# Attention's transposed outputs: copied by ScalarE, scaled by GpSimd, and GpSimd's weight work spread between

## The chip, the cores and the metric

One core of a Trainium2 chip runs the whole program in one launch. The metric is the device time in microseconds; lower is better.

## The reference

The input x has 8 sequences of 256 tokens with 512 features, and so has the context. One layer is computed, all in f32:

```python
x = x + xattn(layernorm(x), ctx, ctx, Wq, Wk, Wv, Wfc, bfc)   # 32 heads of 16, 8 groups of keys and values
x = x + ffn(layernorm(x), ...)                                # 8 experts, the best 2 in 2 of 4 groups, and a shared one

# in xattn, for each head
score = einsum('bhqd,bhkd->bhqk', qh, kh) / sqrt(HEAD_DIM)
attn = softmax(score, axis=-1)
out = einsum('bhqk,bhkd->bhqd', attn, vh)
return out.reshape(N, S_, EMBED) @ Wfc.T + bfc
```

The softmax is where the change lies: the kernel sums the exponentials with a column of ones beside the values, and divides the output by that sum at the end.

## The kernel before

**Stages.** Up to about 103 us in the profile the projections of q, k and v are computed and written to DRAM as pairs of f16 parts. Then comes the attention loop, to about 290 us. Then, tile by tile of 128 tokens (`TILES` is 16), the output projection, the second norm and the gate run. The expert network follows, with the weights held in SBUF as pairs of f16 parts.

**The attention loop.** It has 16 units (4 blocks of 512 tokens by 4 slices of the features, `UNITS`), each with 4 groups G (`UG`). A group is one key head with its four query heads over one sequence of 256 tokens; two groups that follow each other are a pair, so there are 32 pairs, two in each unit. Every engine has its own program over G, and each runs in order:

- TensorE (L1347 to L1385): four score fills per group (`score_fill`, L1304), each into bank 4 or 5; four fills for the row maxima of the unit after the next (`max_fill`, L1232; none in the last two units); the products with the values (`pv_part`, L1318) into bank 6; and in every odd group `pair_transpose(G - 3)` (L1335), four transposes of a finished pair into bank 7. Once per unit the row maxima are transposed into a part of bank 7 too (L1243). A score fill waits for the exp two fills before it.
- ScalarE (L1021 to L1032): four exps per group (L1028), then `attn_out(G - 1)` (L1014), a copy of a group's output from bank 6 into one of four buffers, `o_raw`.
- VectorE (L1854 to L1880): two reductions per group for the row maxima (`reduce`, L1701), the negated maxima once per unit (`neg_max_part`, L1758, L1761), and in every odd group `normalise(G - 3)`: the reciprocals of the sums in bank 7 (L1828) and the multiply of bank 7 by them into `attn_u` (L1830). In the last two units the reductions give way to the largest magnitudes of the down weights (`dn_abs_max`, L1838), each of which waits for a load into one of three ring buffers.
- GpSimd (L844 to L850): ten halves of the expert weights are cut in two f16 parts (`cut_weights`), each by three instructions over 128x1408: scaled and rounded (L818), scaled in place (L801), and the rest (L811); a half waits for `nm_done`, so there is about one per unit. After each comes one of 16 tiles to which the bias is added: `load_x(t + 1)` (L833), the add (L838) and the store (L840). `load_x(t)` waits until the store of tile t - 2 has landed, as they have two buffers. After ten halves the last six tiles follow one on the other.
- SyncE (L521 to L560): for each unit the negated maxima are stored into the q buffer (`nm_rows`, L511), twelve loads bring q and k of a later unit (`load_unit`, L475 and L479), and `store_attn` (L517) writes a finished unit's output to DRAM once `attn_done` says that both its pairs are normalised. From unit 12 on, the ring loads of the down weights (`load_ring`, L460) stand between these, `load_ring(9)` behind `store_attn(14)`. Its queue is in order: a store that waits holds up what stands behind it. At unit 15 the residual rows' load waits until all of one parity's attention stores have landed.

**After the loop** TensorE waits for `attn_done` of all groups (L1388) and begins the output projection of tile 0 (transposes L1397, products L1405). VectorE goes on with the tenth down-weight maximum and then the first tile's sum and norm (L1894 on). GpSimd waits for the last maximum before it loads the held weights (L792).

The functions that the diff touches:

Of the kernel before, what the change touches and what calls it, by code (L numbers as in the profile page):

```python
# [26 lines left out]
ALU = mybir.AluOpType  # L27
# [53 lines left out]
def build(nc, x, ctxT, wqT, wkvT, wfcT, bfc, gwT, wgu, wdn, out):  # L81
# [17 lines left out]
    with ExitStack() as ctx:  # L99
# [53 lines left out]
        assert at <= P3_0  # L153
# [92 lines left out]
        o_rec = small(2 * NM, TPB * HPG).rearrange("p (a h) -> p a h", a=TPB)  # L246
# [98 lines left out]
        ot_ready = sem("ot_ready")  # L345
# [51 lines left out]
        TOTAL = PA + PB + PC  # L397

# [348 lines left out]
        def _(pool):  # L747
# [66 lines left out]
            def cut_weights(c):  # L814
# [4 lines left out]
                scale_weights(c)  # L819
                second_part(c)  # L820
                if c + 2 < CUTS_P2:
                    load_cut(c + 2)
# [21 lines left out]
            for t in range(TILES):  # L844
                if t < CUTS_P2:
                    pool.wait_ge(nm_done, t + 3)
                    cut_weights(t)
                if t + 1 < TILES:
                    load_x(t + 1)
                add_bias(t)  # L850

# [66 lines left out]
        def _(act):  # L918
# [96 lines left out]

            exp_by = [nc.scalar.alloc_register(f"exp_by{n}") for n in range(BLOCKS)]
# [4 lines left out]
            for G in range(UNITS * UG):  # L1021
# [8 lines left out]
                if G > 0:  # L1030
                    attn_out(G - 1)
            attn_out(UNITS * UG - 1)  # L1032

# [140 lines left out]
        def _(pe):  # L1174
# [149 lines left out]
            def pair_transpose(G):  # L1324

                pe.wait_ge(pv_evac, G + 2)
                if G == 0:
                    pe.wait_ge(scale_done, 1)
                else:
                    pe.wait_ge(attn_done, G)  # L1330
# [16 lines left out]
            for G in range(UNITS * UG):  # L1347
# [22 lines left out]
                if j == 0 and has_next:  # L1370
                    if G > 0:
                        pe.wait_ge(attn_done, G - 2)
# [15 lines left out]
            pe.wait_ge(attn_done, LAST + 1)  # L1388
# [254 lines left out]
        def _(dve):  # L1643
# [177 lines left out]
            def normalise(G):  # L1821

                u, g = G // UG, G % UG // UB
                dve.wait_ge(ot_ready, G // 2 + 1)
                if g == 0:
                    dve.wait_ge(attn_st[u % 2], u // 2 * 16 + FREE)
                src = bank[7].rearrange("p (a h c) -> p a h c", a=TPB, c=VW)
                nc.vector.reciprocal(o_rec, src[:, :, :, HD]).then_inc(rec_done, 1)  # L1828
                dve.wait_ge(rec_done, G // 2 + 1)
                nc.vector.tensor_tensor(  # L1830
                    attn_u[u % 2][:, :, g * HPG * HD:(g + 1) * HPG * HD].rearrange("p a (h d) -> p a h d", d=HD),
                    src[:, :, :, 0:HD], o_rec.unsqueeze(3).broadcast_to([P, TPB, HPG, HD]),
                    ALU.mult).then_inc(attn_done, UB)
# [636 lines left out]
```

## Time and profile before

| what | us |
|---|---|
| median of 3 runs | 791.03 |
| lowest and highest run | 786.33 and 792.75 |
| the profiled execution | 788.99 |
| its span in the trace | 787.2 |
| TensorE, VectorE, ScalarE, GpSimd busy | 752.7, 580.6, 412.7, 269.9 |

The profiled execution's time is the span and 1.8 us around it. Busy time of TensorE is modelled, so a high share does not say that it runs at its peak. The mean granted clock of TensorE was 0.993 of full speed.

### The profile page before, as it was taken

To read this page: it belongs to the slowest core of one execution; us is meant where nothing else is said; L and a number is where in the kernel's file an instruction comes from. 1 tells how busy PE (TensorE), PEld (TensorE's weight loads), DVE (VectorE), ACT (ScalarE), POOL (GpSimd) and SP (SyncE) were. 2 spreads that over 40 slices of the span, in tenths; PEclk is the share of its full clock that TensorE was granted. 3 is DMA by queue.
4 is the path that set the end of the run, shared out by engine and by line. 5 is a ranking of instruction groups with operands and counts; after the bars stand their busy time and mean duration, and the time that the engine had idled before them with its cause. 6 is when DMAs were issued, how large, how long until landed. Compare 5 with 4: busy or idle time off the path is not lost.

```text
span 787.2 us, 15941 instructions
## 1 busy us (share of the span) xinstructions
PE 752.7 (96%) x5151; PEld 406.3 (52%) x5152; DVE 580.6 (74%) x1194; ACT 412.7 (52%) x843; POOL 269.9 (34%) x224
## 2 busy tenths in 40 slices
PE   6998989999998989999999999999999999998997
PEld 4553534344333335655655655555555555554553
DVE  5767789899998876999789886555555555545667
ACT  3665578798888863555534553343434334232231
POOL 3362008999993302556100101111111111033431
PEclk9999999999999999999999999999999999999999
DMA  8998856656646799996678566776777777569985
GB/s 318 358 394 239 251 159 207 188 158 206 188 123 181 261 330 324 333 386 219 184 240 228 124 148 156 173 186 174 177 177 176 184 173 176 124 194 255 276 246 152
DMA packets 161784, 172.09 MB, mean 219 GB/s; under 512 B 103680, under 2 KB 117504, under 8 KB 161216
## 3 DMA queue, kind: packets, MB, share of 16 engines
q1 hardware_dynamic: 150012, 128.89, 56.9%
q0 software_dynamic: 11120, 41.43, 17.3%
q10 hardware_dynamic: 596, 1.07, 0.4%
q8 instruction: 31, 0.51, 0.3%
q14 instruction: 25, 0.20, 0.1%
HBM read 105.40 MB, written 42.73 MB: 188 GB/s over the span
## 4 chain that ended last, share of the span: by engine, by line
PE 64%; DVE 16%; DMA 8%; SPq 4%; issue 4%; ACT 2%; ACTq 0%; DVEq 0%
PE psum L1469 28%; PE psum L1481 15%; PE psum L1318 6%; PE psum L1304 4%; PE psum L1208 4%; PE psum L1232 3%; DMA sb_weights<-k_parts 2%; DMA sb_hT<-sb_h 2%; DMA sb_weights<-in_wdn 2%; SPq L475 2%; PE psum L1405 1%; DVE sb_rows L1904 1%; SPq L479 1%; DVE sb_rows L1701 1%; DVE sb_stats L1896 1%
## 5 line engine op out<-in xcount | busy, mean ns | idle before, releaser
L1469 PE MATMUL psum<-sb_weights,sb_rows 128*128 (+1 forms) x1608 | 251.7, 313 | 0.0
L1469 PEld LDWEIGHTS psum<-sb_weights,sb_rows 128*128 128x128 f16 x1608 | 157.6, 98 | 92.1 <-issue 0.5
L1701 DVE TENSOR_REDUCE sb_rows<-psum 128x4 f32<-128x1024 f32 x128 | 150.4, 1215 | 9.9 <-PE psum L1232 9.8
L1028 ACT ACTIVATE sb_weights<-psum 128x512 f32<-128x512 f32 x256 | 139.8, 595 | 27.7 <-PE psum L1304 24.8
L1481 PE MATMUL psum<-sb_weights,sb_hT 128*128 (+1 forms) x630 | 148.3, 381 | 3.3 <-DMA sb_hT<-sb_h 3.3
L892 POOL DMA_INDIRECT sb_rows<-xn_rows,sb_slot_tok x39 | 38.4, 984 | 218.3 <-DVE sb_rows L2290 147.8
L1481 PEld LDWEIGHTS psum<-sb_weights,sb_hT 128*128 128x128 f16 x630 | 61.5, 98 | 68.9 <-DMA sb_hT<-sb_h 4.1
L1097 ACT ACTIVATE psum<-psum 128x352 f32<-128x352 f32 x71 | 31.8, 448 | 113.5 <-DVE psum L1951 113.5
L1304 PE MATMUL psum<-sb_weights 50*128 50x512 f16 x256 | 86.3, 386 | 2.7 <-ACT sb_weights L1028 1.4
L1318 PE MATMUL psum<-sb_weights 128*32 128x256 f32 x1024 | 82.5, 395 | 0.3
L1232 PE MATMUL psum<-sb_weights 48*128 48x256 f16 x512 | 69.9, 273 | 5.2 <-DMA sb_weights<-k_parts 4.4
L912 POOL DMA_INDIRECT sb_weights<-slot_y,sb_p_i x32 | 31.8, 995 | 83.7 <-DMA slot_y<-sb_rows 39.8
L1951 DVE SCALAR_TENSOR_TENSOR psum<-psum,sb_inv_now,sb_h 128x352 f32<-128x352 f32 x39 | 23.1, 593 | 49.3 <-PE psum L1469 49.3
L1405 PE MATMUL psum<-sb_weights 128*128 128x512 f32 x128 | 58.9, 603 | 0.1
L1964 DVE SCALAR_TENSOR_TENSOR sb_h<-psum,sb_h_scale_i,sb_h 128x352 f16<-128x352 f32 x71 | 41.3, 582 | 18.8 <-ACT sb_h L1102 18.6
L1304 PEld LDWEIGHTS psum<-sb_weights 50*128 50x128 f16 x256 | 23.4, 93 | 55.1 <-ACT sb_weights L1028 43.8
L1092 ACT ACTIVATE sb_h<-psum,sb_inv_now 128x352 f32<-128x352 f32 x39 | 21.6, 553 | 55.5 <-PE psum L1469 55.5
L1208 PE MATMUL psum<-sb_weights 128*128 128x512 f16 x192 | 44.9, 380 | 3.9 <-issue 2.6
L1102 ACT ACTIVATE sb_h<-psum,sb_h_scale_i 128x352 f16<-128x352 f32 x71 | 39.3, 553 | 17.6 <-DVE sb_h_scale_i L1956 17.6
L801 POOL TENSOR_TENSOR sb_weights<-sb_weights,sb_w_scale_i 128x1408 f32<-128x1408 f32 x15 | 38.5, 2570 | 27.7 <-ACT sb_weights L1070 26.9
L1092 ACT ACTIVATE sb_h<-psum,sb_w_inv_i 128x352 f32<-128x352 f32 x32 | 17.7, 554 | 54.2 <-PE psum L1469 40.4
L811 POOL TENSOR_TENSOR sb_weights<-sb_weights 128x1408 f16<-128x1408 f32 x15 | 42.9, 2859 | 1.2
(266 smaller groups left out, 1018.2 us busy)
## 6 DMA issues: line engine op xcount, KB each, us to landing
sb_weights<-in_wgu SPq DMA_DIRECT2D x20, 704.0 KB, 7.6
sb_weights<-in_wgu POOLq DMA_DIRECT2D x20, 704.0 KB, 5.6
sb_weights<-in_wdn SPq DMA_DIRECT2D x17, 768.0 KB, 5.7
slot_y<-sb_rows SPq DMA_DIRECT2D x39, 256.0 KB, 2.3
sb_weights<-q_parts SPq DMA_DIRECT2D x96, 64.0 KB, 2.5
x_dram<-sb_rows SPq DMA_DIRECT2D x24, 256.0 KB, 4.3
q_parts<-sb_weights SPq DMA_DIRECT2D x16, 256.0 KB, 4.4
sb_rows<-in_x POOLq DMA_DIRECT2D x16, 256.0 KB, 4.6
```

Of the source, the lines that this page charges most:

```text
L811: nc.gpsimd.tensor_tensor(low, stage, high, ALU.subtract).then_inc(gu_cut, 1)
L1028: nc.scalar.activation(probs[G % 2][:, kt, pair * 512:(pair + 1) * 512], bank[4 + f % 2], ACT.Exp, scale=exp_by[n]).then_inc(exp_done, 1)
L1092: nc.scalar.activation(silu_out[par], two_parts(bank[GU_BANKS[par][0]]), ACT.Silu, scale=inv).then_inc(sil_done, 1)
L1208: mm = nc.tensor.matmul(bank[Q_BANKS[n][m]], wq16[:, wp, k, m * P:(m + 1) * P], xnT[n % 2][:, xp, k, :], start=(k == 0 and i == 0), stop=( ...
L1232: mm = nc.tensor.matmul(bank[banks[qt] + side][:, h * SEQ:(h + 1) * SEQ], q_st[s][lo:hi, g, h, b * SEQ + qt * P:b * SEQ + (qt + 1) * P], k ...
L1304: nc.tensor.matmul(bank[4 + side].rearrange("p (h t) -> p h t", h=HH), k_st[s][lo:hi, g, b * SEQ + kt * P:b * SEQ + (kt + 1) * P], q_st[s] ...
L1318: mm = nc.tensor.matmul(bank[6][VW * c:VW * (c + 1), 0:SEQ], v_now, probs[G % 2][:, kt, c * SEQ:(c + 1) * SEQ], start=(kt == 0), stop=(kt ...
L1405: mm = nc.tensor.matmul(bank[2 + s][:], oT[s][:, k, :], wfc_sb[:, k, :], start=(k == 0), stop=(k == KD - 1))
L1469: mm = nc.tensor.matmul(bank[GU_BANKS[par][which]][:, 0:F], x_T[:, xp * D + k * P:xp * D + (k + 1) * P], gu(wp, k, which), start=(k == 0 a ...
L1481: mm = nc.tensor.matmul(bank[Y_BANKS[par]][:], hT[par][:, hp, j, :], dn(wp, j), start=(j == 0 and n == 0), stop=(j == NF - 1 and n == 2))
L1701: nc.vector.tensor_reduce(to[:, :, j // UB, :, j % UB, qt], psum[:, banks[qt] * 512:(banks[qt] + 2) * 512] .rearrange("p (a h k) -> p a h ...
L1964: nc.vector.scalar_tensor_tensor(h16[par][:, 1, 0:F], bank[GU_BANKS[par][1]][:, 0:F], h_scale[:, par:par + 1], h16[par][:, 0, 0:F], ALU.mu ...
```

## The change

ScalarE copies bank 7 whole, after a pair's transposes, into one of two new SBUF buffers `o_t` (`copy_pair`). VectorE takes the reciprocals from there, into one of two small buffers (`sums`), a group later than before. GpSimd multiplies (`normalise`). TensorE waits for the copy, where it waited for the normalised pair. GpSimd's 30 cut steps and 16 bias tiles are placed by a table between the multiplies: two or three steps and one or no tile per unit up to unit 12, then three tiles in unit 13, four in unit 14.

```diff
+        o_t = [words(at + s * D, D).rearrange("p (a h c) -> p a h c", a=TPB, c=VW) for s in range(2)]
-        o_rec = small(2 * NM, TPB * HPG).rearrange("p (a h) -> p a h", a=TPB)
+        o_rec = [small(at, TPB * HPG).rearrange("p (a h) -> p a h", a=TPB) for at in (2 * NM, 424)]
+        PAIRS = UNITS * UG // UB
...
# GpSimd
+            def cut_step(i):
+                c = i // 3
+                if i % 3 == 0:
+                    first_part(c)
+                elif i % 3 == 1:
+                    scale_weights(c)
+                else:
+                    second_part(c)
+                    if c + 2 < CUTS_P2:
+                        load_cut(c + 2)
+            def normalise(p):
+                u, g = p // MG, p % MG
+                pool.wait_ge(rec_done, p + 1)
+                pool.wait_ge(ot_copied, p + 1)
+                if g == 0:
+                    pool.wait_ge(attn_st[u % 2], u // 2 * 16 + FREE)
+                nc.gpsimd.tensor_tensor(
+                    attn_u[u % 2][:, :, g * HPG * HD:(g + 1) * HPG * HD].rearrange("p a (h d) -> p a h d", d=HD),
+                    o_t[p % 2][:, :, :, 0:HD], o_rec[p % 2].unsqueeze(3).broadcast_to([P, TPB, HPG, HD]),
+                    ALU.mult).then_inc(attn_done, UB)
...
-            for t in range(TILES):
-                if t < CUTS_P2:
-                    pool.wait_ge(nm_done, t + 3)
-                    cut_weights(t)
-                if t + 1 < TILES:
-                    load_x(t + 1)
-                add_bias(t)
+            done_cuts = done_bias = 0
+            for u in range(UNITS):
+                cuts = (3 if u in (2, 5, 8, 11) else 2) if u < 13 else 0
+                biases = {2: 0, 5: 0, 8: 0, 11: 0, 13: 3, 14: 4, 15: 0}.get(u, 1)
+                for i in range(cuts):
+                    if i == 1 and u > 0:
+                        normalise(2 * u - 1)
+                    cut_step(done_cuts)
+                    done_cuts += 1
+                if cuts == 0:
+                    normalise(2 * u - 1)
+                for i in range(biases):
+                    if done_bias + 1 < TILES:
+                        load_x(done_bias + 1)
+                    add_bias(done_bias)
+                    done_bias += 1
+                normalise(2 * u)
+            normalise(PAIRS - 1)
...
# ScalarE
+            def copy_pair(p):
+                act.wait_ge(ot_ready, p + 1)
+                if p >= 2:
+                    act.wait_ge(attn_done, UB * (p - 1))
+                nc.scalar.copy(o_t[p % 2], bank[7].rearrange("p (a h c) -> p a h c", a=TPB, c=VW)).then_inc(ot_copied, 1)
                 if G > 0:
                     attn_out(G - 1)
+                if G % 2 == 1 and G > 2:
+                    copy_pair((G - 3) // 2)
             attn_out(UNITS * UG - 1)
+            copy_pair(PAIRS - 1)
...
# TensorE: pair_transpose, the maxima's transpose, after the loop
-                    pe.wait_ge(attn_done, G)
+                    pe.wait_ge(ot_copied, G // UB)
-                        pe.wait_ge(attn_done, G - 2)
+                        pe.wait_ge(ot_copied, (G - 2) // UB)
-            pe.wait_ge(attn_done, LAST + 1)
+            pe.wait_ge(ot_copied, PAIRS)
...
# VectorE
+            def sums(p):
+                dve.wait_ge(ot_copied, p + 1)
+                if p >= 2:
+                    dve.wait_ge(attn_done, UB * (p - 1))
+                nc.vector.reciprocal(o_rec[p % 2], o_t[p % 2][:, :, :, HD]).then_inc(rec_done, 1)
-                if j % 2 == 1 and G > 2:
-                    normalise(G - 3)
+                if j % 2 == 0 and G > 3:
+                    sums((G - 4) // 2)
...
+            sums(PAIRS - 2)
             dn_abs_max(2 * UG)
-            normalise(UNITS * UG - 2)
+            sums(PAIRS - 1)
             dn_abs_max(2 * UG + 1)
```

## Rows read from the trace of the kernel before

**Rows 1.** Busy time by stretch: stretch, length, engines, TensorE clock, DMA share, GB/s
```profile
115.00:260.00 145.00, 140.03 (x1518) 56.72 (x1518) 135.79 (x177) 122.61 (x250) 119.37 (x83) 0.99 0.60 177
260.00:289.00 29.00, 27.46 (x258) 9.84 (x254) 23.57 (x28) 24.75 (x51) 4.21 (x5) 1.00 0.94 328
```

**Rows 2.** Timeline of ScalarE in the last two units: start, length, instruction, idle before
```profile
273.63 2.31 ACT L1028 ACTIVATE sb_weights<-psum 128x512 f32<-128x512 f32 x4
...
276.67 2.16 ACT L1028 ACTIVATE sb_weights<-psum 128x512 f32<-128x512 f32 x4 [0.46 <-PE psum L1304]
...
279.12 2.31 ACT L1028 ACTIVATE sb_weights<-psum 128x512 f32<-128x512 f32 x4
...
286.80 0.38 ACT L1014 COPY sb_rows<-psum 128x256 f32<-128x256 f32 x1
```

**Rows 3.** Timeline of ScalarE, one unit with row maxima
```profile
229.58 0.38 ACT L1014 COPY sb_rows<-psum 128x256 f32<-128x256 f32 x1
230.42 2.20 ACT L1028 ACTIVATE sb_weights<-psum 128x512 f32<-128x512 f32 x4 [0.47 <-PE psum L1304]
...
240.56 0.38 ACT L1014 COPY sb_rows<-psum 128x256 f32<-128x256 f32 x1
```

**Rows 4.** Timeline of TensorE, a pair's transposes and the fill behind
```profile
229.41 0.66 PE L1335 MATMUL psum<-sb_ident,sb_rows 128*128 128x128 f32 x4
230.00 0.39 PE L1304 MATMUL psum<-sb_weights 50*128 50x512 f16 x1
```

**Rows 5.** Timeline of SyncE's queue in the attention loop
```profile
119.04 1.06 SPq L511 DMA_DIRECT2D sb_weights<-sb_rows  x2
...
130.02 1.05 SPq L511 DMA_DIRECT2D sb_weights<-sb_rows  x2
...
136.71 0.42 SPq L517 DMA_DIRECT2D attn_dram<-sb_rows  x1
...
222.95 1.05 SPq L511 DMA_DIRECT2D sb_weights<-sb_rows  x2
...
258.22 1.05 SPq L511 DMA_DIRECT2D sb_weights<-sb_rows  x2
...
269.68 1.05 SPq L511 DMA_DIRECT2D sb_weights<-sb_rows  x2
```

**Rows 6.** Timeline of VectorE, one pair's normalisation and the reductions behind
```profile
225.12 0.23 DVE L1828 RECIPROCAL sb_rows<-psum 128x16 f32<-128x16 f32 x1
225.45 0.42 DVE L1830 TENSOR_TENSOR sb_rows<-psum,sb_rows 128x256 f32<-128x256 f32 x1
```

**Rows 7.** Timeline of ScalarE, copies of 128x512 out of PSUM
```profile
304.84 0.58 ACT L1044 COPY sb_rows<-psum 128x512 f32<-128x512 f32 x1
305.30 0.60 ACT L1038 COPY sb_weights<-psum 128x512 f32<-128x512 f32 x1
```

**Rows 8.** Timeline of GpSimd, the first weight half and bias tile
```profile
120.00 2.53 POOL L818 TENSOR_TENSOR sb_weights<-sb_weights,sb_w_scale_i 128x1408 f16<-128x1408 f32 x1 [2.90 <-DMA sb_weights<-in_wgu]
...
125.23 2.87 POOL L811 TENSOR_TENSOR sb_weights<-sb_weights 128x1408 f16<-128x1408 f32 x1
128.39 0.59 POOL L789 DMA_DIRECT2D sb_weights<-in_wgu  x1 [0.30 <-POOL sb_weights L811]
128.98 0.54 POOL L833 DMA_DIRECT2D sb_rows<-in_x  x1
129.53 1.29 POOL L838 TENSOR_TENSOR sb_rows<-sb_rows,sb_weights 128x512 f32<-128x512 f32 x1
...
131.71 2.55 POOL L818 TENSOR_TENSOR sb_weights<-sb_weights,sb_w_scale_i 128x1408 f16<-128x1408 f32 x1
```

**Rows 9.** Timeline of GpSimd, bias tiles after the last weight half
```profile
238.44 0.54 POOL L833 DMA_DIRECT2D sb_rows<-in_x  x1 [2.36 <-DMA xb_dram<-sb_rows]
...
243.89 0.54 POOL L833 DMA_DIRECT2D sb_rows<-in_x  x1 [2.76 <-DMA xb_dram<-sb_rows]
```

**Rows 10.** The page's DMA issues: line, queue, count, size each, median to landing
```profile
sb_rows<-in_x POOLq DMA_DIRECT2D x16, 256.0 KB, 4.6
```

**Rows 11.** Timeline of TensorE, the first transposes of the output projection
```profile
292.04 1.97 PE L1397 MATMUL psum<-sb_ident,sb_weights 128*128 128x128 f32 x8 [2.47 <-DVE sb_rows L1830]
```

**Rows 12.** Busy time by stretch, around the end of the attention loop
```profile
292.00:294.00 2.00, 1.96 (x9) 1.66 (x9) 1.72 (x1) 0.59 (x1) 0.00 (x0) 0.52 0.79 243
```

More of the change, by code:

```diff
@@ L152, in build @@
         at += 4 * k_words
-        assert at <= P3_0
+        o_t = [words(at + s * D, D).rearrange("p (a h c) -> p a h c", a=TPB, c=VW) for s in range(2)]
+        assert at + 2 * D <= P3_0
         x_in = [words(at + s * TPB * D, TPB * D).rearrange("p (a d) -> p a d", a=TPB) for s in range(3)]
@@ L344, in build @@
         max_ready, max_done, mxt_ready = sem("max_ready"), sem("max_done"), sem("mxt_ready")
-        ot_ready = sem("ot_ready")
+        ot_ready, ot_copied = sem("ot_ready"), sem("ot_copied")
         nm_first, nm_done, rec_done = sem("nm_first"), sem("nm_done"), sem("rec_done")
@@ L812, in second_part, with first_part @@
                 pool.wait_ge(gu_cut, pool_cuts(c))
-            def cut_weights(c):
+            def first_part(c):
                 stage, scale = scaled_weights(c)
@@ L818, in cut_weights @@
                 nc.gpsimd.tensor_tensor(high, stage, scale.broadcast_to([P, HALF]), ALU.mult).then_inc(gu_first, 1)
[L819 to L822, printed above, removed]
+            def cut_step(i):
[18 more added lines that the diff above has]
+                    ALU.mult).then_inc(attn_done, UB)
             pool.wait_ge(kq_ready, KQ * BLOCKS)
@@ L843, in _ @@
             load_x(0)
-            for t in range(TILES):
-                if t < CUTS_P2:
-                    pool.wait_ge(nm_done, t + 3)
-                    cut_weights(t)
-                if t + 1 < TILES:
-                    load_x(t + 1)
-                add_bias(t)
+            done_cuts = done_bias = 0
[16 more added lines that the diff above has]
+            normalise(PAIRS - 1)
+            assert done_cuts == 3 * CUTS_P2 and done_bias == TILES
             def dn_second(e, count, pieces):
@@ L1819, in _ @@
             links = first_link.count[0]
[L1821 to L1833, printed above, removed]
+            def sums(p):
[3 more added lines that the diff above has]
+                nc.vector.reciprocal(o_rec[p % 2], o_t[p % 2][:, :, :, HD]).then_inc(rec_done, 1)
             def dn_abs_max(i):
```

## The prediction

> **What bounds the kernel now.** I first asked where in the span the change lies. The attention loop runs from about 103 to 289 us. The page's first part has TensorE busy 96% of the span, as modelled, which tells little here. The stretch table shows VectorE busy 135.8 of 145 us there and ScalarE 122.6, then, in the last 29 us, where no more row maxima are taken, VectorE at 23.6 and GpSimd nearly idle [rows 1]. By busy share VectorE looks like the bound, and taking 0.42 us per pair off it looks like a gain. The next view says otherwise. ScalarE's timeline in that last part, with only the ring maxima left on VectorE, repeats from 273.63 to 279.12, 5.49 us per pair of groups [rows 2]. In the part with row maxima one unit (two pairs) takes 229.58 to 240.56, 10.98 us, so again 5.49 per pair [rows 3]. Removing 4.9 us of VectorE reductions per pair changes nothing: the loop is set by the exchange between TensorE (score fill) and ScalarE (exp), not by VectorE. In a group without transposes ScalarE never idles: 276.67 to 279.12, 2.45 us for four exps and one copy. In the other it waits 0.46 us for TensorE, because the four transposes stand in front of the next score fill: they start at 229.41, the fill at 230.00, and ScalarE continues at 230.42 [rows 2 to 4].
>
> The loop's other loss is the q and k loads. SyncE's marks (one per unit, where it stores the negated maxima) run from 119.04 to 269.68 in 13 steps; 13 x 10.98 would be 142.7, so 7.9 us go to units that wait for loads. From mark to the attention store behind the twelve loads it is 6.7 us [rows 5].
>
> **The change part by part.** VectorE: per pair the 0.42 us multiply and its wait go, the reciprocal stays [rows 6]. As VectorE sets no pace, I value this at nothing. If it did bind, it would be worth 0.4 x 28 = 11 us at most; that is the other end.
>
> ScalarE: 32 copies of 128x512 from PSUM are added. Such a copy lasts 0.58 us and the next instruction begins 0.46 later [rows 7]; I take 0.49. The copy of pair p stands behind the same group's transposes, so it starts when they end, at 229.41 + 0.66 = 230.07, inside the idle time. The next exp could start at 230.07 + 0.03 + 0.49 = 230.59 instead of 230.42: 0.17 us per pair, 0.33 per unit. Bounds: 0 (all in the idle 0.46) and 0.49. Over 13 units it is 4.3 us (0 to 13). The wider step gives each late load 0.33 more: of the 7.9 us lost in 13 steps, six of which lost over 0.33, about 2.5 come back.
>
> GpSimd: no row shows the multiply of 128x256. Nearest are the 128x512 add, 1.29 us, and the 128x1408 scaling with a broadcast factor, 2.53 us, 1.8 ns per element [rows 8]. By element that is 0.46 to 0.65; with a fixed part I take 0.7, and keep 0.46 and 1.29 as ends. The Trainium skill (GPSIMD Engine Reference, Performance versus the Vector engine) says that a tensor_tensor takes 1.96 times as long as on VectorE; by that the estimate is 0.83 per multiply instead of 0.7, and the sum grows by 0.5 us. The trace of before has no multiply of this shape on GpSimd, but the add is in line with the page.
>
> Now GpSimd's queue, in order. A cut step takes 2.6 us, the third 3.2, and 0.6 for the next load's issue; a bias tile 2.7 (load issue, add, 0.3 wait, store issue) [rows 8]. A unit of two steps, one bias and two multiplies comes to about 10.4, against 11.3 for the loop: it fits, barely. It starts late, though: the first load arrives at 120.00 [rows 8]. Unit 0's list (two steps, a bias, multiply 0) ends at 128.7, while ScalarE's copy of pair 2, which waits for multiply 0, wants to run at 127.4: 1.3 us. Multiply 1 then stands behind a third step (3.7) and ends at 133.1. SyncE's store of that unit waits for it, and behind that store in SyncE's queue stand the next maxima and twelve loads, which went at 130.02 [rows 5] and now go at 133.5. The loads already came late there, so up to 3.5 us fall on the path; part of it coincides with the copies' shift and part returns at the next late load. I take 2 (0 to 3.5). Unit 13's mark then comes 4.3 - 2.5 + 2 = 3.8 us after the 258.22 of before [rows 5], at 262.0.
>
> The tail decides. Seven of the sixteen bias tiles are placed in units 13 (three) and 14 (four), in front of multiplies 26 and 28. Two buffers serve them, so the load of tile t+1 waits until the store of tile t-1 has landed. Where no weight work lay between (from 238 us) this gives a cycle of 5.45 us, 238.44 to 243.89, of which about 2.8 is the wait; not the 2.7 of the bias alone [rows 9]. Counted from unit 13's mark: VectorE took the reciprocals of such a pair 2.2 after the mark (225.12 against 222.95 [rows 5, 6]) and now takes them a group (2.8) later; with 0.8 for multiply 25 and its signal it ends at +5.8. Tile 9 needs 2.7, tiles 10 and 11 5.5 each, multiplies 26 and 27 0.7 each: +20.9. Tile 12 4.1 (the multiplies cover part of the wait), tiles 13 and 14 5.5 each, tile 15 4.6 (its load lands 4.6 after issue by the median [rows 10]), multiply 28 0.7: +41.3, or 303.3. ScalarE's copy of pair 30 waits for multiply 28, because both use the same one of two buffers. It would be due after the last exps, which ended at 286.80, 28.6 after the mark [rows 2], now about 29.4. So ScalarE stands 12 us. Behind that copy in its queue is the copy of the last group's output, on which the last transposes wait; then these (0.7), the copy of pair 31 (0.6) and signals: TensorE begins the output projection 2.6 after 303.3, at 305.9. It began at 292.04, after 2.47 us waiting for VectorE's last normalisation, behind a down-weight maximum [rows 11]; that wait goes, but it is replaced by the larger one. The difference is +13.9. Beside this, SyncE's store for unit 14 and the last down-weight load behind it also wait for multiply 29, so the last maximum comes at about 312, just as the first projected tile (6.3 after TensorE's start, 312.2): late together, no further loss. Everything after keeps its order, and I add nothing there.
>
> On the clock: after the 2.5 us in which TensorE stood still the granted clock fell to 0.52, the 1.2 GHz level, in 292 to 294 [rows 12]. The longer idle time ends in the same low stretch, which is paid already. The Trainium skill (TensorE: Matmul & The Clock Gate, HAM oscillation) likewise has idle time between bursts throttle the clock; by it the four last transposes may run slow too, 0.3 us more.
>
> Sum: 3.8 to unit 13's mark and 10.1 in the tail, 13.9 in all. The profiled execution took 788.99 us (span 787.2 and 1.8 around it): 802.9. The median of the runs, 791.03, lies 2 above it. I forecast 804.
>
> **The rivals.** No change, decided at the tail: if a bias tile in units 13 and 14 took under 3.6 us, multiply 28 would end before +29.4 and the copy of pair 30 would find it done. Left are the 3.8 us of the loop, less 2.65 for TensorE's earlier start: 792. For it: while weight work lay between them, tiles did not wait and took 2.7 [rows 8]. Against: the cycle of 5.45 is that of tiles alone [rows 9], and in the tail the loads of the down weights compete with it.
>
> Faster: the loads' 7.9 us are cured, since the store's new place and the wider step shift them off their limit, copies vanish in the 0.46 idle, and the tail binds no one: 791 - 7.9 - 2.65 = 780. It needs the tail rival's condition as well, and that no load is late any more, where 7.9 us in 13 steps were lost [rows 5].
>
> Slower still: the multiply, with rows of 16 elements, costs 1.29 or more on GpSimd. A unit of its list is then 11.6, above 11.3, so GpSimd sets the pace of the first 13 units (+4), and the tail's four multiplies add 2.4; with tile cycles of 6 us another 2: 812.
>
> **How the numbers follow.** Forecast 60%; slower still 17%; no change 17%; faster 6%. My own range is 799 to 809: tile cycles of 5.0 to 6.0, copies at 0 to 0.49, start 0 to 3.5. The full range reaches toward both neighbours, 795 to 812. A measurement of this kernel can tell about 1% (8 us) from no change. So faster by over 1% has 6%, within 1% 17%, slower 77%.
>
> **What would show it.** Right: ScalarE's pair period at about 5.65 with the idle before the even group's exps gone; one long ScalarE wait for a GpSimd multiply at about 290 to 303, with GpSimd alternating bias tiles and waits for its own store there; TensorE idle for over 12 us before the line that transposes the attention rows; the mark after 130 delayed by 2 to 3.5. Wrong: that wait under 4 us, a pair period of 5.49 or less, or multiplies above 1.2 us with ScalarE waiting all along the loop. If bias tiles cycle in under 4 us in the tail, the forecast fails with it.

## The result, and the profile after

| | kernel before | changed kernel |
|---|---|---|
| median, us | 791.89 (4 runs on the same chip) | 815.84 (814.23 to 824.45, 4 runs) |
| profiled execution, its span | 788.99, 787.2 | 817.25, 815.5 |
| mean granted clock of TensorE | 0.993 | 0.969 |

The ratio on record is 1.0376, 95% interval 1.0327 to 1.0425; the two medians of the table alone give 1.030, as the four runs of the kernel before beside it came out high. In later runs beside the experiments its medians were 788.13, 787.11 and 787.55, and every ratio below is to the runs of the kernel before that stand beside that experiment. The sign is the forecast's; the size is not: 804 was predicted, with a range that ended at 812.

Where the 28.3 us of span lie is read off three places. SyncE's mark of unit 13 stands at 268.87, where it was 258.22 [rows 5]: +10.65. TensorE's first transposes of the output projection start at 319.54, where it was 292.04 [rows 11]: +27.5, so the tail added 16.85. From there to the end the remaining 0.8 is added. SyncE's queue in the attention loop of the changed kernel (start, length, instruction):

```profile
122.16 1.06 SPq L513 DMA_DIRECT2D sb_weights<-sb_rows  x2
...
135.52 0.38 SPq L519 DMA_DIRECT2D attn_dram<-sb_rows  x1
135.98 1.05 SPq L513 DMA_DIRECT2D sb_weights<-sb_rows  x2
...
148.01 1.05 SPq L513 DMA_DIRECT2D sb_weights<-sb_rows  x2
...
159.33 1.05 SPq L513 DMA_DIRECT2D sb_weights<-sb_rows  x2
...
170.66 1.05 SPq L513 DMA_DIRECT2D sb_weights<-sb_rows  x2
...
176.84 0.42 SPq L481 DMA_DIRECT2D sb_weights<-k_parts  x1
...
184.92 1.05 SPq L513 DMA_DIRECT2D sb_weights<-sb_rows  x2
...
268.87 1.05 SPq L513 DMA_DIRECT2D sb_weights<-sb_rows  x2
```

Two units run at 11.33 (148.01, 159.33, 170.66), which is the 10.98 + 0.33 of the forecast; the next takes 14.26, and so do others nearly: the thirteen steps from 122.16 to the last mark at 280.15 (the row that answers to 269.68 of [rows 5]) take 157.99, 10.7 more than 13 x 11.33, where the kernel before lost 7.9 over its own pace.

ScalarE's timeline (start, length, instruction, idle before and its releaser), which answers to [rows 2] and [rows 3]:

```profile
276.19 0.58 ACT L1054 COPY sb_weights<-psum 128x512 f32<-128x512 f32 x1
276.68 2.17 ACT L1068 ACTIVATE sb_weights<-psum 128x512 f32<-128x512 f32 x4
...
281.85 0.59 ACT L1054 COPY sb_weights<-psum 128x512 f32<-128x512 f32 x1
...
286.99 0.38 ACT L1047 COPY sb_rows<-psum 128x256 f32<-128x256 f32 x1
293.07 0.58 ACT L1054 COPY sb_weights<-psum 128x512 f32<-128x512 f32 x1 [5.70 <-POOL sb_rows L841]
...
305.86 0.38 ACT L1047 COPY sb_rows<-psum 128x256 f32<-128x256 f32 x1
316.83 0.58 ACT L1054 COPY sb_weights<-psum 128x512 f32<-128x512 f32 x1 [10.60 <-POOL sb_rows L841]
```

A pair takes 5.66 (276.19 to 281.85). The copy now stands where the 0.46 of idle time stood, and the exps follow 0.49 behind its start. Then two copies wait for multiplies of GpSimd: pair 28's 5.70 and pair 30's 10.60. The forecast had one such wait, of 12. GpSimd's timeline, same columns, answers to [rows 9]:

```profile
174.67 0.58 POOL L791 DMA_DIRECT2D sb_weights<-in_wgu  x1 [0.30 <-POOL sb_weights L813]
...
274.40 0.58 POOL L855 DMA_DIRECT2D sb_rows<-in_x  x1
...
280.66 0.54 POOL L855 DMA_DIRECT2D sb_rows<-in_x  x1 [3.52 <-DMA xb_dram<-sb_rows]
...
289.64 0.54 POOL L855 DMA_DIRECT2D sb_rows<-in_x  x1 [6.28 <-DMA xb_dram<-sb_rows]
...
292.35 1.20 POOL L841 TENSOR_TENSOR sb_rows<-sb_weights,sb_rows 128x256 f32<-128x256 f32 x2
...
304.74 0.54 POOL L855 DMA_DIRECT2D sb_rows<-in_x  x1 [7.44 <-DMA xb_dram<-sb_rows]
...
311.09 0.54 POOL L855 DMA_DIRECT2D sb_rows<-in_x  x1 [3.65 <-DMA xb_dram<-sb_rows]
...
316.12 1.20 POOL L841 TENSOR_TENSOR sb_rows<-sb_weights,sb_rows 128x256 f32<-128x256 f32 x2
```

Before a tile is loaded, GpSimd waits up to 7.4 us for the store two tiles back. The tiles' loads go out at 274.40, 280.66, 289.64, 294.55, 304.74 and 311.09: 7.3 apart on average, where the forecast took 5.5 from the quieter stretch of [rows 9]. What else stood waiting then is seen in the waits of 100 to 320 us (engine, line, releaser: us, times, longest) and in the busy time by stretch (TensorE, weight loads, VectorE, ScalarE, GpSimd; then the granted clock, the DMA share, GB/s), which answers to [rows 1] and [rows 12]:

```profile
POOL sb_rows L855 <- DMA xb_dram<-sb_rows: 21.9, 5, 7.4
ACT sb_weights L1054 <- POOL sb_rows L841: 18.2, 3, 10.6
...
DVE sb_dn_max L1874 <- DMA sb_weights<-in_wdn: 13.5, 5, 8.2
...
PE psum L1378 <- ACT sb_rows L1047: 11.0, 2, 10.3
```

```profile
150.00:171.00 21.00, 20.65 (x227) 8.21 (x224) 18.98 (x24) 19.90 (x42) 18.74 (x17) 1.00 0.59 183
171.00:198.00 27.00, 25.08 (x241) 9.63 (x240) 20.52 (x24) 21.72 (x44) 19.12 (x14) 0.87 0.53 134
...
290.00:302.00 12.00, 7.50 (x45) 2.21 (x45) 0.92 (x2) 6.86 (x14) 5.64 (x8) 0.57 0.76 252
302.00:319.00 17.00, 6.36 (x54) 2.60 (x53) 6.97 (x6) 5.06 (x12) 8.40 (x11) 0.76 0.61 221
```

The down-weight loads, due in the same 290 to 302, came late as well (VectorE stood 8.2 us for one). SyncE's queue shows why: four of them stood behind the attention store that waited for GpSimd's multiply 27. When it was done, three went out within 1.0 us, and the fourth at 303.9, when a ring buffer was free.

```profile
281.25 1.01 SPq L462 DMA_DIRECT2D sb_weights<-in_wdn  x2
293.58 0.38 SPq L519 DMA_DIRECT2D attn_dram<-sb_rows  x1
...
295.53 8.68 SPq L462 DMA_DIRECT2D sb_weights<-in_wdn  x4
```

And behind each stall TensorE's granted clock went to its lower level: 0.57 of full speed on average in 290 to 302, so mostly 1.2 GHz.

TensorE's own side of the second stall, timeline rows that answer to [rows 11]:

```profile
317.75 1.12 PE L1378 MATMUL psum<-sb_ident,sb_rows 128*128 128x128 f32 x4 [10.29 <-ACT sb_rows L1047]
319.54 1.97 PE L1440 MATMUL psum<-sb_ident,sb_weights 128*128 128x128 f32 x8 [0.67 <-ACT sb_weights L1054]
```

The last pair's transposes took 1.12, where four such took 0.66 at full clock [rows 4]. Two questions stayed open: what the tail's tiles were worth by themselves, and why the loop had lost 10.65 where 3.8 was forecast.

### The profile page after: what moved, and what is told of

It is laid out like the page before. It is cut to its first block, busy times and chain, and to the rows that moved or that the text cites. A ratio compares the mean times of both kernels' runs of the same rounds, so it can differ in the third digit from the quotient of the medians.

```text
span 815.5 us, 16023 instructions
## 1 busy us (share of the span) xinstructions
PE 765.9 (94%) x5151; PEld 409.6 (50%) x5152; DVE 572.4 (70%) x1162; ACT 429.1 (53%) x875; POOL 288.3 (35%) x256
## 4 chain that ended last, share of the span: by engine, by line
PE 64%; DVE 12%; DMA 10%; issue 5%; ACT 4%; POOL 2%; SPq 2%; another core or an unknown queue 0%; ACTq 0%; DVEq 0%; POOLq 0%
PE psum L1512 28%; PE psum L1524 15%; PE psum L1361 5%; PE psum L1251 4%; PE psum L1347 3%; DMA xb_dram<-sb_rows 3%; PE psum L1275 3%; DMA sb_rows<-xb_dram 2%; ACT sb_weights L1068 2%; PE psum L1378 2%; DMA sb_hT<-sb_h 1%; POOL sb_rows L860 1%; PE psum L1448 1%; DMA sb_weights<-k_parts 1%; DMA sb_weights<-in_wqT 1%
## 5 line engine op out<-in xcount | busy, mean ns | idle before, releaser
L1744 DVE TENSOR_REDUCE sb_rows<-psum 128x4 f32<-128x1024 f32 x128 | 153.3, 1213 | 23.0 <-PE psum L1275 22.5
L1347 PE MATMUL psum<-sb_weights 50*128 50x512 f16 x256 | 88.3, 405 | 11.8 <-ACT sb_weights L1068 9.6
L1361 PE MATMUL psum<-sb_weights 128*32 128x256 f32 x1024 | 87.1, 414 | 0.8
L1275 PE MATMUL psum<-sb_weights 48*128 48x256 f16 x512 | 75.1, 282 | 3.5 <-DMA sb_weights<-k_parts 3.0
```

The source lines that it names most:

```text
L1275: mm = nc.tensor.matmul(bank[banks[qt] + side][:, h * SEQ:(h + 1) * SEQ], q_st[s][lo:hi, g, h, b * SEQ + qt * P:b * SEQ + (qt + 1) * P], k ...
L1347: nc.tensor.matmul(bank[4 + side].rearrange("p (h t) -> p h t", h=HH), k_st[s][lo:hi, g, b * SEQ + kt * P:b * SEQ + (kt + 1) * P], q_st[s] ...
L1361: mm = nc.tensor.matmul(bank[6][VW * c:VW * (c + 1), 0:SEQ], v_now, probs[G % 2][:, kt, c * SEQ:(c + 1) * SEQ], start=(kt == 0), stop=(kt ...
L1744: nc.vector.tensor_reduce(to[:, :, j // UB, :, j % UB, qt], psum[:, banks[qt] * 512:(banks[qt] + 2) * 512] .rearrange("p (a h k) -> p a h ...
```

## The experiments

**One tile per unit.** The changed kernel with the 16 bias tiles spread evenly:

```diff
-                biases = {2: 0, 5: 0, 8: 0, 11: 0, 13: 3, 14: 4, 15: 0}.get(u, 1)
+                biases = 1
```

> The changed kernel with one bias tile in every unit instead of three in unit 13 and four in unit 14. Theory A (the tiles queued in the tail, each waiting for its own store, make ScalarE wait for multiplies 26 and 28): the two long ScalarE waits (5.7 and 10.6 us) go, TensorE's start into the output projection comes 16 to 20 us earlier, about 798 us in all. Rival B (GpSimd's list as a whole is too long for the loop): nothing is gained, since the same tiles now lengthen the first thirteen units; the waits move forward and the time stays at 812 or more. Theory A allows a few short ScalarE waits at the start.

Measured: 803.23 us (800.06 to 803.94), ratio to the kernel before 1.0183, interval 1.0137 to 1.0229; 12.6 us under the changed kernel, where the expectation had 798. The long waits of ScalarE for multiplies are gone, and the projection's transposes begin at 304.48, 15.1 earlier (16 to 20 was expected): from unit 13's mark (271.63) it is 32.9 instead of 50.7, but the mark itself comes 2.8 later. Part of the price comes back behind them, since the last tile is now stored last. TensorE's timeline of this kernel:

```profile
309.44 5.87 PE L1448 MATMUL psum<-sb_weights 128*128 128x512 f32 x8 [3.87 <-ACT sb_weights L1081]
```

ScalarE's copy for that product had itself waited 4.38 for a tile's store to land. Without that wait the move might be worth more; no run tried it.

**Four buffers for the last tiles.** The changed kernel's order of work is kept, but the tiles of the tail get two more buffers and are loaded two ahead:

```diff
...
-                nc.gpsimd.dma_start(xb_sb[t % 2], x_tiles[t]).then_inc(xb_ld[t % 2], 16)
+                nc.gpsimd.dma_start(xb_all[b], x_tiles[t]).then_inc(xb_ld_all[b], 16)
...
-                    if done_bias + 1 < TILES:
-                        load_x(done_bias + 1)
+                    for ahead in {9: (10, 11), 10: (12,), 11: (13,), 12: (14,), 13: (15,), 14: (), 15: ()}.get(done_bias, (done_bias + 1,)):
+                        load_x(ahead)
```

> The changed kernel, same order of work, but the last tiles use four buffers instead of two and are loaded two ahead, so that a load never waits for the store before it. Theory A: tiles in the tail take 3 to 4 us each instead of 5 to 10, the ScalarE waits shrink from 16.3 us to under 4, the time falls to 798 to 803. Rival B (the number of instructions in GpSimd's list): no change, 814 to 817. Rival C (transfers of the down weights slow every tile whatever its buffers): the tiles still cycle at 5 us or more, 808 or more.

Measured: 802.12 us (800.78 to 806.46), ratio 1.0197, interval 1.0147 to 1.0247; 13.7 under the changed kernel. ScalarE's waits for multiplies in its tail, of the copies of pairs 30 and 31:

```profile
300.06 0.58 ACT L1064 COPY sb_weights<-psum 128x512 f32<-128x512 f32 x1 [1.73 <-POOL sb_rows L843]
302.88 0.58 ACT L1064 COPY sb_weights<-psum 128x512 f32<-128x512 f32 x1 [1.97 <-POOL sb_rows L843]
```

Pair 28's wait of 5.70 is gone, pair 30's fell from 10.60 to 1.73, with the same seven tiles in the same place: the price was in the wait for the buffers, not in the additions. The 1.97 is a new wait, of pair 31's copy for multiply 29, which started at 302.17 behind VectorE's reciprocals of 301.80; these stood behind down-weight maxima that waited for their loads. From unit 13's mark (268.51) to the projection (303.52) it is 35.0 us, against 50.7 in the changed kernel and 33.8 before. The tail is settled; +10 at the mark is left.

**The multiply back on VectorE, from the SBUF copy.** ScalarE copies as in the change; VectorE takes reciprocal and multiply, and GpSimd does what it did before:

```diff
...
+                dve.wait_ge(rec_done, p + 1)
+                nc.vector.tensor_tensor(
+                    attn_u[u % 2][:, :, g * HPG * HD:(g + 1) * HPG * HD].rearrange("p a (h d) -> p a h d", d=HD),
+                    o_t[p % 2][:, :, :, 0:HD], o_rec[p % 2].unsqueeze(3).broadcast_to([P, TPB, HPG, HD]),
+                    ALU.mult).then_inc(attn_done, UB)
```

> ScalarE copies as in the change, but VectorE takes reciprocals and multiplies, from the copy, and GpSimd's weight work and tiles stand in the order of the kernel before. What stays of the change is the copy and the shorter waits of TensorE. My theory: the pair period is 5.66 us as in the changed kernel (ScalarE's copy sets it), so 0.17 x 32 = 5 us over the kernel before, less some of the late loads' time: 792 to 797. Rival: if most of the 10.6 us lost before unit 13 came from the copy by way of more late loads and low clock, 798 to 802. If VectorE's relief had been what the copy pays for, this loses it and is slower than the changed kernel without its tail.

Measured: 796.06 us (794.67 to 798.35), ratio 1.0111, interval 1.0070 to 1.0153. So the copies and what goes with them cost 1.1% without any work on GpSimd. The time is in the expected range, the pace is not: 5.66 per pair was expected, but a unit takes 11.76 us in this kernel, not 11.33, and its waits between 115 and 290 us name why:

```profile
PEld psum L1271 <- DVE sb_rows L1740: 9.8, 20, 3.1
```

TensorE's fills for the row maxima wait for VectorE's reductions 20 times. One unit took 15.32 (224.91 to 240.23), with the longest of these waits in it, 3.1, so a part of the 1.1% is VectorE's as well. With the copies making everything a little later and the multiply still there, VectorE is at its limit (the forecast's busy share of 135.8 in 145 us was that near). Taking the multiply off VectorE is thus worth some 0.4 us per unit, but only once the copies have been added, as this comparison of 11.76 and 11.33 suggests.

**Almost no multiply.** The kernel before with VectorE's multiply cut to one of 16 columns; it leaves 15/16 of the attention's output unwritten (the output buffers are filled with zeros once, at the start):

```diff
...
-                    src[:, :, :, 0:HD], o_rec.unsqueeze(3).broadcast_to([P, TPB, HPG, HD]),
+                    src[:, :, :, 0:1], o_rec.unsqueeze(3),
```

> The kernel before with VectorE's multiply cut to one of 16 columns: leaves out 15 of 16 parts of attention's output scaling, VectorE gains about 0.25 us per pair. My theory (VectorE does not set the loop's pace): pair period 5.49 us as before, the time within 2 us of the kernel before. Rival (VectorE at 94% busy is what the loop waits for): 0.25 x 28 = 7 us faster, 784, with a pair period of 5.25.

Measured: 788.97 us (785.56 to 791.68, 10 runs), ratio 0.9999, interval 0.9972 to 1.0026. Its groups of VectorE (busy us, mean ns) show that the cost is really gone: the multiply fell from 425 ns in the kernel before to

```profile
L1832 DVE TENSOR_TENSOR sb_rows<-psum,sb_rows 128x16 f32<-128x16 f32 x32 | 5.9, 185 | 3.3
```

7.7 us of VectorE bought nothing: the rival's 784 would be a ratio of 0.995, outside the interval. In the kernel before, VectorE does not set the pace.

**Four buffers, and the attention store one unit later.** On the kernel with four buffers:

```diff
                 load_unit((u + 3) // KD, (u + 3) % KD)
-                store_attn(u - 1)
+                if u >= 2:
+                    store_attn(u - 2)
+            store_attn(UNITS - 5)
```

> The four-buffer kernel (802.1 us) with SyncE's store of a unit's attention output placed one unit later, so that it never waits for GpSimd's multiply. Theory: the second mark no longer waits (13.8 us from mark 1 to mark 2 becomes 11.3 to 12), 1.5 to 3 us faster than the four-buffer kernel: 799 to 801. Rival: the wait is hidden, as the q and k loads come late for another reason: 802.

Measured: 800.28 us (799.32 to 808.05, 5 runs), ratio 1.0161, interval 1.0108 to 1.0215: 1.8 below four buffers alone. That is the time that the theory expected, but it lies inside the spread of either kernel, and the step that should have shrunk did not: the unit that the store was thought to hold back takes 16.24 us (120.42 to 136.66), where four buffers alone took 13.83. The profiled execution, at 808.05, was the slowest of the five, so its numbers are an upper end. Its ScalarE timeline names another cause:

```profile
131.46 0.59 ACT L1066 COPY sb_weights<-psum 128x512 f32<-128x512 f32 x1 [3.85 <-POOL sb_rows L845]
```

The copy of pair 2 waits for multiply 0 directly. In the changed kernel the same wait is 1.91. There the store of 135.52 had waited 6.5 us for multiply 1, and the negated maxima for which the mark at 135.98 waits were ready at 135.95: the two came together, and the profile names the maxima as the releaser, as for 13 of its marks. So SyncE's store cannot be what held the start: without it the mark would have come no earlier.

**The weight load behind the bias tile.** On the kernel with four buffers; the load of the next weight half (704 KB), which the third cut step issues, is held until the unit's bias tile is done:

```diff
                     second_part(c)
-                    if c + 2 < CUTS_P2:
-                        load_cut(c + 2)
...
+                if held_load is not None:
+                    load_cut(held_load)
+                    held_load = None
                 normalise(2 * u)
```

> The four-buffer kernel with the load of the next weight half (704 KB) issued after the unit's bias tile instead of right after the third cut step. In the changed kernel the units with steps of 13 to 14 us are those where this load was issued 3 to 4 us after a mark, among the q and k loads. Theory D (the change moved that load onto the q and k loads, these land 4.2 instead of 2.1 us after issue, TensorE waits and its clock falls): the long units go, marks 2 to 13 lie within 11.3 to 12.3 apart, 3 to 6 us faster than the four-buffer kernel: 796 to 799. Rival (late loads are the twelve issues in SyncE's queue alone): no change, 802.

Measured: 796.56 us (795.54 to 797.48), ratio 1.0118, interval 1.0064 to 1.0172; 5.6 under four buffers alone (800.78 to 806.46), as expected. Its SyncE marks between 159.91 and 274.89:

```profile
159.91 1.05 SPq L515 DMA_DIRECT2D sb_weights<-sb_rows  x2
...
171.66 1.05 SPq L515 DMA_DIRECT2D sb_weights<-sb_rows  x2
...
182.98 1.05 SPq L515 DMA_DIRECT2D sb_weights<-sb_rows  x2
...
274.89 1.05 SPq L515 DMA_DIRECT2D sb_weights<-sb_rows  x2
```

Ten units take 114.98, only 1.7 over 10 x 11.33; with four buffers alone the same ten took 123.69 (156.11 to 279.80) and in the changed kernel 120.82 (159.33 to 280.15). Of the 8.7 gained on the first, 2.5 went back in the three units ahead of them. The four-buffer kernel and the changed kernel, with the same order of work in those ten units, differ by 2.9 already, so the times are the better measure of the gain.

In the changed kernel the weight load went out at 174.67, 188.91 and 235.93, 4.0 us behind a mark, among the twelve q and k loads; those units took 14.26, 13.04 and 13.88, and the last k load of the first of them, issued at 176.84, landed 4.20 later. The longest landing of a k load was 4.3 to 4.4 in each of these three units and at most 3.7 in the other nine from 122.16 to 268.87. In the kernel with the load moved, one is still in that place, at 138.14, 3.5 behind the mark at 134.67: a k load took 5.0 and the unit 13.92, against the expectation that all from the second mark on would stay under 12.3. Over the six kernels with the change's order of GpSimd's work, every weight load issued 3.5 to 4.7 us behind a mark, 14 in all, stands in a unit of 12.8 to 15.8; some units without one were long as well (up to 12.8 behind the first three). The kernel before issued its weight loads 8 to 11 us behind a mark, after those loads. With the load moved, the granted clock of the stretch that had 0.87 in the changed kernel is full:

```profile
171.00:184.00 13.00, 12.82 (x145) 5.05 (x144) 11.91 (x16) 12.19 (x26) 10.35 (x8) 1.00 0.36 93
```

**The first multiply early.** On the kernel of the last experiment, multiply 0 directly behind the first cut step:

```diff
-                    if i == 1 and u > 0:
-                        normalise(2 * u - 1)
+                    if i == 1:
+                        normalise(2 * u - 1 if u > 0 else 0)
```

> The changed kernel with four buffers for the last bias tiles and the weight load behind the bias tile (796.56 us), and with multiply 0 issued straight behind GpSimd's first weight step instead of behind two steps and a bias tile. Theory: the two long units that remain at the start (14.5 and 13.9 us) come from ScalarE, whose copy of the third pair waited 2.10 us for multiply 0 at 129.48, and from TensorE, whose clock stood at 0.53 of full speed in 132:138 behind that wait. With multiply 0 at about 123.5 no copy waits for it: the second and third step fall to 11.5 to 12.5 each, the granted clock in 132:138 is near 1.00, and the time is 791 to 794. Rival: the long steps are landings of late loads, and ScalarE's wait lies beside them: the wait goes, but the steps stay at 13.5 or more, and the time is 795 to 798.

Measured: 799.17 us (794.25 to 800.34), ratio 1.0125, interval 1.0079 to 1.0170: no gain over 796.56 (ratio 1.0118), and above even the rival's 795 to 798. The wait and the low clock behind it are gone (busy time by stretch of this kernel):

```profile
132.00:138.00 6.00, 5.93 (x71) 2.42 (x67) 5.67 (x8) 5.71 (x13) 5.84 (x5) 1.00 0.27 75
```

The second step fell from 14.47 to 13.14, but the third rose to 15.75, for another reason, in TensorE's timeline:

```profile
146.51 0.61 PE L1290 MATMUL psum<-sb_weights 48*128 48x256 f16 x4 [4.22 <-DMA sb_weights<-k_parts]
```

The weight load went out at 139.47 in this kernel, 4.7 behind the mark at 134.75: at the start GpSimd's work is not yet in step with the units, and the collision is there again. From 163.25 on, ten units take 114.28, as in the kernel before (114.41). The longest landing of a k load in this unit was 5.5. That the late k load has its cause in the weight load agrees with the last experiment, but was not tried for this one place.

**The loads ahead of the maxima's rows.** On the kernel before, SyncE's twelve loads go ahead of the rows of negated maxima:

```diff
-                nm_rows(u + 1)
                 sp.wait_ge(pv_ready, u * UG)
                 load_unit((u + 3) // KD, (u + 3) % KD)
+                nm_rows(u + 1)
```

> The kernel before with SyncE's twelve q and k loads ahead of the negated maxima instead of behind them: they start some 2.6 us earlier in each unit. Theory: the marks come 10.98 us apart in all units, the 7.9 us of late loads go, and the low clock after them: 6 to 8 us faster than before, 780 to 783. If VectorE or the exchange of TensorE and ScalarE took up the gain elsewhere: under 3 us.

Measured: 789.57 us (783.68 to 795.01, 10 runs), ratio 1.0024, interval 0.9987 to 1.0061: no gain. The waits between 115 and 290 us show what took its place:

```profile
PEld psum L1304 <- DMA sb_weights<-sb_rows: 9.8, 11, 1.6
PE psum L1304 <- DMA sb_weights<-sb_rows: 6.5, 9, 1.4
```

Now the score fills wait for the rows of maxima, in place of the maxima's fills waiting for k. The loads themselves now wait for the products of the unit that leaves the buffer (SyncE, 12 times, 54.2 us in all), which bounds how early they can start.

**The same, with the projection not waiting for the last pair.**

```diff
-            pe.wait_ge(attn_done, LAST + 1)
+            pe.wait_ge(attn_done, LAST - 1)
```

> As the kernel with the loads first, and TensorE begins the output projection without waiting for VectorE's last normalisation (it waits for the pair before). Theory: TensorE's idle 2.5 us at 289.6 falls under 1 and its clock stays high, but VectorE's first sum still stands behind the last down-weight maximum (294.0 before): 2 to 4 us faster than the loads alone. If the maximum's load sets the end of the loop: no gain.

Measured: 787.39 us (784.28 to 794.96, 10 runs), ratio 1.0003, interval 0.9967 to 1.0040. It is 2.2 us under the last one by the medians, but the intervals overlap widely, so that the 2 to 4 us expected are not shown; it is level with the kernel before.

**The projection earlier, alone.** The edit just shown, by itself on the kernel before.

> The kernel before, with only one edit: TensorE starts the output projection when all but the last pair are normalised. Theory: the first four transposes read rows of earlier units, so the 2.47 us at 292.04 is a wait for nothing that they need: the projection starts some 2.5 us earlier, the granted clock in 292:294 is not halved, and the time falls 2 to 4 us, ratio 0.995 to 0.998. Rival: what follows is bound by the loads of the residual rows and by VectorE's first sums, which come when they did: the wait moves behind the transposes, and the ratio is 0.999 to 1.001.

Measured: 786.47 us (782.81 to 790.04, 12 runs) against 787.55, ratio 0.9978, interval 0.9956 to 1.0000. It is the one version that may be ahead of both kernels; the interval ends at no difference, and the rival's ratio of 0.999 is inside it. The tail does what the theory said (TensorE's timeline and busy time by stretch of this kernel, to be held against [rows 11] and [rows 12]):

```profile
292.27 0.63 PE L1335 MATMUL psum<-sb_ident,sb_rows 128*128 128x128 f32 x4 [0.55 <-ACT sb_rows L1014]
292.73 1.04 PE L1397 MATMUL psum<-sb_ident,sb_weights 128*128 128x128 f32 x8
```

```profile
292.00:294.00 2.00, 1.50 (x12) 1.29 (x12) 1.23 (x2) 0.70 (x3) 0.00 (x0) 1.00 1.06 413
```

From unit 13's mark to the projection's transposes it is 31.2 (261.55 to 292.73), 2.6 less than before, the granted clock stays at full speed, and the transposes take 1.04 instead of 1.97. The span of this execution, 788.3, is no shorter, as its start was slow: the mark that answers to the 119.04 of [rows 5] came at 123.00.

## Why the prediction was right or wrong

**VectorE's relief at nothing: right.** With 7.7 of its 13.6 us cut away the ratio was 0.9999. The rival "faster" did not rest on this but on cured loads and a tail that binds no one: more was lost to late loads than before, and the tail bound.

**ScalarE's copies, 0.17 us per pair: right.** The pair period is 5.66 (forecast 5.65 or so), a unit 11.33, and the idle in front of the even group's exps is filled by the copy. Over the 12 steps to unit 13's mark that is 4.2. What the copies cost in all is at most the 1.1% of the kernel with the copies alone, as VectorE's limit adds to it there.

**GpSimd's multiply at 0.7: right enough.** It took 0.62 on average over 32. Against 0.7 this gives back under 0.4 us in the tail. The rival "slower still", which wanted 1.29, had a time nearer the result than the forecast's, but for a reason that did not occur. By the ratio of 1.96 in the Trainium skill (GPSIMD Engine Reference, Performance versus the Vector engine) the estimate from VectorE's 0.425 was 0.83; the measured ratio is 1.46, and the measurement decides.

**The loop up to unit 13, +3.8: wrong, the first failed step.** It measured +10.65. The forecast's three terms were copies +4.3, late loads -2.5, and +2 at the start. The marks part the measured number as follows: +3.1 is there at the first mark already; the copies cost 4.2, which came; the first three units lost 3.2 over the pace of 11.33, as before over 10.98 (3.3); and the nine units behind (159.33 to 268.87) lost 7.6, where the kernel before lost 4.1 (155.27 to 258.22). So the term that failed is that of the late loads: more than 3 us were added to them where 2.5 were to come back. The +2 of the start is not found in the first three units' sum.
- The late loads. The forecast let the wider step loosen the q and k loads and looked at nothing else in the queues. But the change also moved the issue of the 704 KB weight loads, which ran in step with the units, 8 to 11 us behind each mark, to wherever the third cut step falls among the multiplies. In three of ten units that was in the middle of the q and k loads, whose landings then took up to 4.4: a transfer that nobody waits for made others late. The rival, that ScalarE waited there for late multiplies, does not hold: between 100 and 320 us it waited for one only three times (1.91, 5.70 and 10.60), never in these units. Held back by one bias tile, the load's move gave 5.6 us, and then the relief forecast does show: ten units lose 1.7 to loads where the kernel before lost 4.6 (155.27 to 269.68, 114.41 against 10 x 10.98).
- The start. A cost was forecast through SyncE's store, and postponing the store left that unit at 16.24 us. The 1.3 us by which multiply 0 was late for ScalarE's copy were in the forecast's own working and were the real path (1.91 in the changed kernel, 2.10 and 3.85 in others). Taken away, the step in question shortens by 1.3, but another late load follows. The +2 did not last: the first step of the changed kernel took 13.82, 2.84 more than before, as forecast, but the first three together (122.16 to 159.33) took 37.2 against 36.2, which is no more than their three units' share of the copies. What the start costs where it does last (39.7 for three units in the kernel with the weight load moved) is only partly settled.
- Chance. 3.1 of the 10.65 are there at the first of these marks already, 122.16 against 119.04. That is no effect of the change that could be shown: TensorE's clock was 0.57 in 106 to 114 in this execution and 1.00 in the one of before, but it was 0.57 and the mark 123.00 in the kernel that differs from the one before only behind the loop, and the changed kernel with four buffers had 1.00 and 118.89.

**The tail, +10.1: right mechanism, mis-sized term.** Measured +16.85. ScalarE's copies do wait for multiplies behind bias tiles that wait for their own stores, and more buffers take 13.7 us away, an even spread 12.6. The term that was mis-sized is the cycle of a tile, 5.5 by a stretch in which no ring load was under way; it measured 4.9 to 10.2, with a mean of 7.3. [rows 1] had shown the DMA share at 0.94 in just these 29 us against 0.60 before them, and the argument that the down-weight loads compete had been used only against the rival "no change". The stores for which GpSimd waited landed 3.8, 6.6, 2.5, 7.7 and 3.9 after their issue. The two long ones, issued at 282.80 and 296.74, went out within 1.6 of two and three ring loads of 768 KB (from 281.25 and 295.53 on); for the others the nearest ring load was issued 3 to 10 us ahead. That these loads are the cause fits all five, but no run moved them. Five cycles, each 1.8 longer on average, make 9 us; 6.75 more than forecast was measured, because the last tile's load landed after 2.8 where 4.6 was taken, and the multiplies were shorter. Because the cycle was longer, multiply 26 was late as well, for pair 28's copy: a stall that the forecast did not have.

**The clock.** The forecast let the low clock behind the stall count as paid by the one of before. There were two stalls and behind each a low stretch (0.57 on average in 290 to 302, 0.76 in 302 to 319), against the one of before [rows 12]. The last transposes were 0.46 longer (0.3 was allowed for); what the rest cost was not separated from the stalls.

**After the loop nothing: right,** within 0.8 us.

**The sum.** 13.9 on the profiled 788.99 gives 802.9, and on the median 804.9; the 804 that was written down lies between the two.

Summed up for the runs: 815.8 for the change, 802.1 without the tail's waits for buffers, 796.6 with the weight load out of the way of q and k. The 9 us that then remain over the kernel before are in part the start (39.7 for three units, where it took 36.2) and in part a tail 1.7 longer (35.6 from unit 13's mark at 263.60 to the projection at 299.16); no version of the change tried here is as fast as the kernel before.

## What to carry to other kernels

When work moves to an engine that also issues transfers, list what else its queue issues and at which moment each transfer now goes out: a large load that nobody waits for can make small ones late that everybody waits for. Take the cycle of a double-buffered load and store from a stretch with the large transfers that it will meet, not from a quiet one. And relief for an engine that is 94% busy can be worth nothing, which one kernel without the relieved work shows at once.

## What the runs showed of the hardware that was not expected

- A GpSimd multiply of 128x256 with a factor broadcast along rows of 16 took 0.62 us, 1.46 times VectorE's 0.425 from PSUM; with both operands in SBUF and short rows it took no more per element than the plain 128x512 add at 1.28.
- TensorE's granted clock in 106 to 114 us differs between executions of nearly the same program: 1.00 in the kernel before and with four buffers, 0.57 in the changed kernel and in the one with the projection earlier, 0.71 with almost no multiply. The first marks of these came at 119.04, 118.89, 122.16, 123.00 and 120.15: up to 4 us later with the lower clock, as much as most of the effects studied. So marks are compared here as differences and times as medians.
- A 32 KB load of k, with a 704 KB load issued 2 us ahead of it on another queue, took 4.20 us to land; the median of the k loads in the loop was 2.3.
